# Out-degree counts folded chunk by chunk and the flag's matmul moved ahead of the last gates, in a two-layer graph kernel

## The chip, the cores and the metric

The kernel runs on one core of a Trainium2 chip. The metric is the device time of one execution in microseconds (us), as the median of several runs. The engines are named as in the profile: PE is TensorE (PEld its weight loads), DVE is VectorE, ACT is ScalarE, POOL is GpSimd, SP is the engine whose queue issues the DMAs.

## What is computed

The reference is two residual graph layers on 6250 nodes with 128 features and 206250 edges, sorted by destination. Cut to what matters:

```python
h = relu(layernorm(x))
deg = segment_sum(ones, src)                    # out-degree
x = x + relu(segment_sum((h * clip(deg, 1) ** -0.5)[src], dst)) @ W.T + b
h = relu(layernorm(x))
messages = segment_sum(h[src] @ W_msg.T + b_msg + edge_embed[type], dst)
x = x + gru_cell(messages, h, W_ih, W_hh, b_ih, b_hh)
```

The edge list holds each drawn edge in both directions and a loop for each node, so every node's out-degree is its in-degree. The kernel uses in-degrees (they are cheap to get from the sorted list) and verifies while it runs that they equal the out-degrees. If they don't, or another assumption on the list fails, a flag is set and a slow general path runs at the end. With these inputs it never runs.

## The kernel before, in words

The nodes are laid out on 125 partitions with 50 nodes each (`BLOCKS`), and the destination nodes are treated in 25 chunks (`CHUNKS`) of two nodes per partition, so 250 destinations (`CH`). For each chunk the kernel builds an adjacency tile in half precision, 50 source blocks by 250 destinations, from one-hot matrices (L698, L1063, L881), multiplies it with the layer's table (L1074) and writes it to a DRAM buffer. That is the first part of the run, up to about 640 us.

Layer 1 (`tensor_layer1`, `scalar_layer1`, `vector_layer1`, `sync_layer1`) reads the adjacency back in the order m = 0 to 24 (the last two chunks, which are still on the chip, come first). Each chunk is loaded into one of two slots of `ring` in four parts (`PARTS`, of 13, 13, 12 and 12 blocks, L417). PE multiplies all 50 blocks, each with a high and a low table (100 matmuls, L1196). Between part 1 and part 2 of chunk m it runs the gate matmuls of chunk m - 1 (`post1_gates_tensor`, L1162 to L1167, single precision), and after part 3 the two transposes of chunk m - 1 (`post1_turn_tensor`, L1173). ACT scales the aggregated messages (L1011) and does the sigmoids (L1018) and the tanh (L1021). DVE does the GRU's elementwise steps: `post1_gate_vector` (L789, L791), `post1_state_vector` (L796, L798, L800) and `post1_out_vector` (L805). SP writes each chunk's result out (L402).

In the same loop DVE adds the chunk's adjacency, part by part, into `counted`, 50 rows of 250 half-precision sums for each partition (`add_counts`, L778). A row belongs to one source node, so the sum over its 250 entries, over all chunks and over the partitions' share is that node's out-degree. The order on DVE is written out by hand: in iteration m the adds of parts 0 and 1 of chunk m, the gate step of chunk m - 1, the add of part 2, the state step of m - 1, the add of part 3, the out step of m - 1. The adds of parts 0 and 1 of the last chunk are pulled to the end of iteration 23. The load of chunk m + 2's part into a slot waits for PE's (`used1`) and DVE's (`added`) use of the part that is there.

After the loop DVE folds the 250 sums of a row to 124, 62 and 32 (L833, three adds), reduces them (L836), compares them with the degrees and collects all flags into `over` (L837 to L844). Only then does it take the gate step of the last chunk. PE has meanwhile done the last chunk's gate matmuls, waits for `mismatch`, sums the flags over the partitions by a one-column matmul (`psFlag`, L1208), and then waits for the last transposes. DVE turns the sum into an integer flag (L847), does the last state step and the last out step. All engines read the flag in `branch` and wait for the output DMAs.

A `Chain` is a helper by which DVE counts its own instructions on a semaphore; `ch.wait()` waits (L112) until all of them so far are done.

Of the kernel before, what the change touches and what calls it, by code (L numbers as in the profile page):

```python
# [7 lines left out]
ALU = mybir.AluOpType  # L8
ACT = mybir.ActivationFunctionType
AX = mybir.AxisListType.X  # L10
# [5 lines left out]
P = slice(0, LO)  # L16
# [3 lines left out]
CH = CB * LO  # L20
CHUNKS = N // CH
# [21 lines left out]
CAND = HLEN + 64  # L43
# [7 lines left out]
PARTS = [(0, 13), (13, 26), (26, 38), (38, BLOCKS)]  # L51
# [10 lines left out]
used0 aggr psX x1 pvar pstd pnm h1 psT hst psM tab_hi psF tab_lo h1T_out  # L62
used1 added h1c_in0 h1c_in1 msg psRZ psN rz nin nn hnew psO result out
load0_0 load0_1 load0_2 load0_3 load1_0 load1_1 load1_2 load1_3
mismatch flag_sum flag_set v_chain
Gflat_in Gx_in Gxb Gh0 Gdeg Gdeg_root Gconst Gtab_zero Gsum_zero Gemb_out Gh0_scaled Gtable_out Gtable1_out
Ghist Ghot Gerows Gturned0 Gturned1 Gsum_in0 Gsum_in1 Gadded0 Gadded1 Gindex Grows0 Grows1 Gsums
Gdiag Gacross Gsame Gproduct
# [50 lines left out]
def gnn(nc, x, edges, dst, dst_heads, w0t, b0, wmt, bm, emb, wiht, whht, bih, bhh, out):  # L119
# [3 lines left out]
    def sem(name):  # L123
        return sems[name]
# [7 lines left out]
    with ctx:  # L132
# [8 lines left out]
        ring = sb("ring", [128, 2, SLOTS * CH], F16)  # L141
# [46 lines left out]
        over = sb("over", [128, CHUNKS], F32)  # L188
# [149 lines left out]
        def slot(m):  # L338
            return (m + 1) % 2
# [428 lines left out]
            post0_x_vector(v, ch, CHUNKS - 2)  # L768
            post0_norm_vector(v, ch, CHUNKS - 2)

        def add_counts(v, m, j):

            a, b = (CH * k for k in PARTS[j])
            part, into = ring[P, slot(m), a:b], counted_n[P, a:b]
            if m >= 2:
                v.wait_ge(sem(f"load{slot(m)}_{j}"), 16 * (m // 2))
                v.wait_ge(sem("added"), 4 * (m - 1) + j + 1)
                v.tensor_tensor(into, into, part, ALU.add).then_inc(sem("added"), 1)  # L778
            elif m == 1:
                v.wait_ge(sem("added"), j + 1)  # L780
                v.tensor_tensor(into, into, part, ALU.add).then_inc(sem("added"), 1)
            else:
                v.tensor_copy(into, part).then_inc(sem("added"), 1)

        def post1_gate_vector(v, ch, m):
            v.wait_ge(sem("psN"), m + 1)
            v.wait_ge(sem("rz"), m + 1)
            positive(v, sem("nn"), m)
            ch.did(v.scalar_tensor_tensor(nin, psN[:, 1, :], bg_h[:, 2:3], rz[:, 0, :], ALU.add, ALU.mult))  # L789
            ch.wait()  # L790
            v.tensor_tensor(nin, nin, psN[:, 0, :], ALU.add).then_inc(sem("nin"), 1)  # L791

        def post1_state_vector(v, ch, m):
            v.wait_ge(sem("nn"), m + 1)
            positive(v, sem("psO"), m)
            ch.did(v.tensor_tensor(hnew, h1c[:, m % 2, :], nn, ALU.subtract))  # L796
            ch.wait()
            ch.did(v.tensor_tensor(hnew, rz[:, 1, :], hnew, ALU.mult))  # L798
            ch.wait()
            v.tensor_tensor(hnew, nn, hnew, ALU.add).then_inc(sem("hnew"), 1)  # L800

        def post1_out_vector(v, m):
            q = chunk(m)
            v.wait_ge(sem("psO"), m + 1)
            v.tensor_tensor(x_sb[P, blocks(q), :], psO, x_sb[P, blocks(q), :], ALU.add).then_inc(sem("result"), 1)  # L805

        def vector_layer1(v, ch):
            last = CHUNKS - 1
            v.wait_ge(sem("built"), UNITS * CHUNKS)
            for m in range(CHUNKS):  # L810
                if m == 0:
                    add_counts(v, m, 0)
                    post0_x_vector(v, ch, last)
                    post0_norm_vector(v, ch, last)
                    for j in range(1, 4):
                        add_counts(v, m, j)
                    check_sorted(v, ch)
                    continue
                if m < last:
                    add_counts(v, m, 0)  # L820
                    add_counts(v, m, 1)
                post1_gate_vector(v, ch, m - 1)
                add_counts(v, m, 2)
                post1_state_vector(v, ch, m - 1)
                add_counts(v, m, 3)
                post1_out_vector(v, m - 1)
                if m == last - 1:
                    add_counts(v, last, 0)
                    add_counts(v, last, 1)

            v.wait_ge(sem("added"), 4 * CHUNKS)
            for to, other in ((124, 126), (62, 64), (32, 32)):
                ch.did(v.tensor_tensor(counted_v[P, :, 0:to], counted_v[P, :, 0:to], counted_v[P, :, other:other + to],  # L833
                                       ALU.add))
                ch.wait()
            ch.did(v.tensor_reduce(outdeg[P, :], counted_v[P, :, 0:32], AX, ALU.add))  # L836
            ch.did(v.tensor_reduce(flags[P, 0:1], over[P, :], AX, ALU.max))  # L837
            ch.did(v.tensor_scalar(flags[P, 3:4], flags[P, 3:4], float(CAND), None, ALU.is_ge))
            ch.wait()
            ch.did(v.tensor_tensor(outdeg[P, :], outdeg[P, :], deg[P, :], ALU.not_equal))  # L840
            ch.wait()
            ch.did(v.tensor_reduce(flags[P, 2:3], outdeg[P, :], AX, ALU.max))
            ch.wait()
            v.tensor_reduce(over[P, 0:1], flags[P, :], AX, ALU.add).then_inc(sem("mismatch"), 1)  # L844
            post1_gate_vector(v, ch, last)
            v.wait_ge(sem("flag_sum"), 1)
            v.tensor_scalar(flag_i[:, :], psFlag, 0.0, None, ALU.is_gt).then_inc(sem("flag_set"), 1)  # L847
            post1_state_vector(v, ch, last)
            post1_out_vector(v, last)

# [303 lines left out]
        def post1_gates_tensor(pe, m):  # L1154
            pe.wait_ge(sem("msg"), m + 1)
            positive(pe, sem("rz"), m)
            positive(pe, sem("nin"), m)
            pe.wait_ge(sem(f"h1c_in{m % 2}"), 16 * (m // 2 + 1))
            h = h1c[:, m % 2, :]
            for a in range(2):  # L1160
                w = slice(D * a, D * (a + 1))
                pe.matmul(psRZ[:, a, :], wih_sb[:, w], msgs, start=True, stop=False)  # L1162
                last = pe.matmul(psRZ[:, a, :], whh_sb[:, w], h, start=False, stop=True)  # L1163
            last.then_inc(sem("psRZ"), 1)
            w = slice(2 * D, 3 * D)
            pe.matmul(psN[:, 0, :], wih_sb[:, w], msgs, start=True, stop=True)  # L1166
            pe.matmul(psN[:, 1, :], whh_sb[:, w], h, start=True, stop=True).then_inc(sem("psN"), 1)  # L1167

        def post1_turn_tensor(pe, m):
            pe.wait_ge(sem("hnew"), m + 1)  # L1170
            positive(pe, sem("result"), m)
            for j in range(CB):
                last = pe.transpose(psO[:, j, :], hnew[:, LO * j:LO * (j + 1)], ident[:, :])  # L1173
            last.then_inc(sem("psO"), 1)
# [3 lines left out]
        def tensor_layer1(pe):  # L1178
            pe.wait_ge(sem("emb_in"), 16 * TA)
            pe.wait_ge(sem("types_moved"), 32)  # L1180
            pe.wait_ge(sem("tab_lo"), CHUNKS - 1)
            for m in range(CHUNKS):
                bank = (CHUNKS + m) % 2
                if m:
                    positive(pe, sem("msg"), m - 1)
                else:
                    pe.wait_ge(sem("aggr"), CHUNKS - 1)
                for j, (a, b) in enumerate(PARTS):
                    if m >= 2:
                        pe.wait_ge(sem(f"load{slot(m)}_{j}"), 16 * (m // 2))  # L1190
                    for h in range(a, b):
                        K = 128 if h < TB else LO
                        if m == 0 and h == CB * (CHUNKS - 1):
                            pe.wait_ge(sem("tab_lo"), CHUNKS)
                        for s in range(2):
                            last = pe.matmul(psD[bank], tabv[1][0:K, h, s, :], adj[slot(m)][0:K, h, :],  # L1196
                                             start=h == 0 and s == 0, stop=h == BLOCKS - 1 and s == 1)
                        if h == b - 1:
                            last.then_inc(sem("used1"), 1)
                        if m == 0 and h in LAST0:  # L1200
                            LAST0[h](pe, CHUNKS - 1)
                    if m and j == 1:
                        post1_gates_tensor(pe, m - 1)
                    if m and j == 3:
                        post1_turn_tensor(pe, m - 1)
            post1_gates_tensor(pe, CHUNKS - 1)
            pe.wait_ge(sem("mismatch"), 1)
            pe.matmul(psFlag, over[P, 0:1], ones[P, 0:1], start=True, stop=True).then_inc(sem("flag_sum"), 1)  # L1208
            post1_turn_tensor(pe, CHUNKS - 1)


# [361 lines left out]
```

## Time and profile before

| | us |
|---|---|
| three runs: median (lowest to highest) | 997.35 (994.53 to 997.53) |
| the profiled execution's own time | 993.72 |
| its span in the profile | 991.9 |
| PE busy | 852.4 (86%) |
| DVE busy | 808.3 (81%) |
| ACT busy | 515.5 (52%) |
| mean granted TensorE clock | 0.975 |

The span is the stretch from the first to the last recorded instruction, and 1.8 us of the execution's own time lie outside it. A granted clock of 1.00 is 2.4 GHz, and 0.50 is 1.2 GHz. In the views below a row of a timeline gives the start, the duration (of all instructions of a merged row together), engine, line, operation, what is written and read, how many (x) and in brackets the idle time of the engine before it with what ended it.

### The profile page before, as it was taken

The page shows a single profiled execution, that of the slowest core. Times are in us where ns is not written, and L with a number is a line of the kernel's source. Part 1 is how long each engine was busy: PE and PEld are TensorE (multiplying, and loading weights), DVE is VectorE, ACT ScalarE, POOL GpSimd, SP SyncE. Part 2 cuts the span into 40 slices and gives each one's busy share as a digit, 9 for nine tenths or more (in the row PEclk, how much of TensorE's full clock was granted, in tenths as well). Part 3 has the DMA queues.
Part 4 walks back from the last instruction along what each step waited for, and adds up shares of the span by engine and source line. Part 5 has one row for each costly group of instructions (what it writes and reads, how often), then busy time and mean ns, then how long its engine had stood idle before and what let it go on. Part 6 is the DMA issues. An engine that isn't in the chain of part 4 may idle for free.

```text
span 991.9 us, 21125 instructions
## 1 busy us (share of the span) xinstructions
PE 852.4 (86%) x8908; PEld 758.8 (77%) x8908; DVE 808.3 (81%) x1177; ACT 515.5 (52%) x1051; POOL 74.4 (8%) x71
## 2 busy tenths in 40 slices
PE   1333599898998998989989999989999999999993
PEld 1222488787887887878878888969888889888882
DVE  5959999999999999999999995267766667766666
ACT  2896278687886886868868887211111111111110
POOL 5860100100101001000000000000000000000000
PEclk9999889999999999999999999999999999999997
DMA  4623315443434544333534330266667776666740
GB/s 108 143 68 130 132 50 221 159 159 136 159 141 159 227 174 159 137 137 147 212 134 187 140 141 7 60 237 242 245 245 266 280 269 245 241 246 260 280 162 12
DMA packets 38739, 169.99 MB, mean 171 GB/s; under 512 B 8156, under 2 KB 21667, under 8 KB 35696
## 3 DMA queue, kind: packets, MB, share of 16 engines
q1 hardware_dynamic: 32486, 161.48, 43.2%
q0 software_dynamic: 6000, 6.48, 2.8%
q8 instruction: 71, 1.16, 0.5%
q10 hardware_dynamic: 154, 0.64, 0.2%
q14 instruction: 28, 0.23, 0.1%
HBM read 88.52 MB, written 80.00 MB: 170 GB/s over the span
## 4 chain that ended last, share of the span: by engine, by line
PE 55%; DVE 29%; ACT 11%; issue 3%; DMA 2%; SPq 0%; DVEq 0%
PE ps L1196 25%; PE ps L1074 13%; DVE work L691 9%; DVE work L698 7%; PE ps L1063 7%; ACT ring L881 5%; DVE work L704 2%; PE ps L1162 2%; PE ps L1163 2%; ACT junk L893 2%; DMA tab<-dst 1%; PE ps L1086 1%; PE ps L1167 1%; PE ps L1166 1%; PE ps L1100 1%
## 5 line engine op out<-in xcount | busy, mean ns | idle before, releaser
L1063 PE MATMUL ps<-work 128*128 128x106 f16 x3125 | 437.2, 217 | 86.4 <-ACT ring L881 66.9
L1074 PE MATMUL ps<-ring,tab 125*128 125x250 f16 x2500 | 422.1, 275 | 1.9 <-DVE tab L676 1.2
L881 ACT ACTIVATE ring<-ps 128x848 f16<-128x848 f32 x375 | 330.0, 882 | 98.1 <-PE ps L1063 92.2
L1063 PEld LDWEIGHTS ps<-work 128*128 128x128 f16 x3125 | 291.4, 102 | 108.0 <-ACT ring L881 67.2
L1196 PE MATMUL ps<-ring,tab 125*128 125x250 f16 (+1 forms) x2500 | 277.0, 269 | 0.0
L1074 PEld LDWEIGHTS ps<-ring,tab 125*128 125x128 f16 x2500 | 246.9, 99 | 28.5 <-DVE tab L676 1.5
L1196 PEld LDWEIGHTS ps<-ring,tab 125*128 125x128 f16 (+1 forms) x2500 | 242.6, 97 | 28.8 <-issue 0.3
L691 DVE TENSOR_TENSOR work<-iota_lo,mch 128x3150 f16<-128x3150 f16 x125 | 224.4, 1795 | 26.0 <-PE ps L1063 13.6
L698 DVE TENSOR_TENSOR work<-iota_w,mch 128x1250 f16<-128x1250 f16 x250 | 193.9, 817 | 0.0
L778 DVE TENSOR_TENSOR work<-work,ring 125x3250 f16<-125x3250 f16 (+1 forms) x92 | 161.8, 1779 | 0.0
L1018 ACT ACTIVATE raw<-ps,bg 128x250 f32<-128x250 f32 x50 | 20.7, 466 | 174.9 <-PE ps L1163 174.9
L789 DVE SCALAR_TENSOR_TENSOR raw<-ps,bg_h,raw 128x250 f32<-128x250 f32 x25 | 11.9, 477 | 96.0 <-PE ps L1167 96.0
L704 DVE TENSOR_TENSOR work<-iota_t,mch_s 128x225 f16<-128x225 f16 x125 | 65.9, 527 | 0.0
L463 POOL DMA_INDIRECT raw<-edges,run_i x25 | 37.6, 1502 | 353.5 <-DVE fields L564 287.5
L1011 ACT ACTIVATE raw<-ps,ginv 128x250 f32<-128x250 f32 x25 | 11.8, 470 | 86.8 <-PE ps L1196 86.8
L921 ACT ACTIVATE h1s<-x_sb,pnm,prs 125x128 f32<-125x128 f32 x50 | 23.9, 482 | 24.1 <-DVE pnm L725 24.1
L456 POOL DMA_INDIRECT ring<-dst,row_i x25 | 33.5, 1342 | 16.0 <-DVE row_i L508 8.7
L1162 PE MATMUL ps<-raw,wih_sb 128*128 128x250 f32 x100 | 29.9, 380 | 3.6 <-DMA raw<-h_turned 3.2
L1021 ACT ACTIVATE raw<-raw,bg_i 128x250 f32<-128x250 f32 x25 | 12.6, 504 | 35.5 <-DVE raw L791 35.5
L1163 PE MATMUL ps<-raw,whh_sb 128*128 128x250 f32 x100 | 29.7, 378 | 0.0
L712 DVE TENSOR_TENSOR x_sb<-ps,x_sb 125x256 f32<-125x256 f32 x25 | 12.2, 490 | 20.2 <-PE ps L1088 20.2
L1086 PE MATMUL ps<-w_sb,aggr 128*125 128x128 f32 x100 | 17.1, 294 | 9.3 <-ACT tab L940 9.3
(156 smaller groups left out, 608.9 us busy)
## 6 DMA issues: line engine op xcount, KB each, us to landing
adjacency<-ring SPq DMA_DIRECT2D x23, 2937.5 KB
ring<-adjacency SPq DMA_DIRECT2D x46, 812.5 KB, 6.3
ring<-adjacency SPq DMA_DIRECT2D x46, 750.0 KB, 8.8
adjacency<-ring SPq DMA_DIRECT2D x23, 183.1 KB
h_turned<-hst SPq DMA_DIRECT2D x25, 125.0 KB, 2.0
raw<-h_turned SPq DMA_DIRECT2D x25, 125.0 KB, 2.0
out<-x_sb SPq DMA_DIRECT2D x25, 125.0 KB
x_sb<-x SPq DMA_DIRECT2D x4, 560.0 KB
```

The lines of the kernel that those rows point to most:

```text
L456: gp.indirect_dma_start(cand[P, g, :], None, dst.rearrange("(a n) -> a n", a=1), bass.IndirectOffsetOnAxis(row_i[P, g:g + 1], 1))\
L463: gp.indirect_dma_start(raw[P, g % RAW, :], None, edges.rearrange("(a n) k -> a (n k)", a=1), bass.IndirectOffsetOnAxis(run_i[P, g:g + 1], ...
L691: ch.did(v.tensor_tensor(lohot[:, s, :, 0:even].rearrange("p k (n t) -> p k n t", t=2), iota_lo[:, 0:even].rearrange("p (n t) -> p n t", t ...
L698: ch.did(v.tensor_tensor(combo[:, s, :, cols].rearrange("p k (n t) -> p k n t", t=2), iota_w[:, cols].rearrange("p (n t) -> p n t", t=2).u ...
L704: v.tensor_tensor(typehot[:, s, :, :, :], iota_t[:, :, :].unsqueeze(1).broadcast_to([128, BATCH, 1 + WIN, TB]), mch_s[:, par, :, at, :].re ...
L778: v.tensor_tensor(into, into, part, ALU.add).then_inc(sem("added"), 1)
L881: act.activation(to(x * 2 * u, 2, x), ps[:, s:s + 2, 0:x * SLOTS].rearrange("p b (x h) -> p h b x", h=SLOTS), ACT.Copy).then_inc(sem("evac ...
L1063: last = pe.matmul(ps[:, 2 * (u % 2) + i // BANKW, o:o + WCOLS], lohot[:, s, k, :], combo[:, s, k, :], start=True, stop=True)
L1074: mm = pe.matmul(psD[c % 2], tabv[0][P, h, s, :], adj[c % 2][P, h, :], start=i == 0, stop=i == 2 * BLOCKS - 1)
L1162: pe.matmul(psRZ[:, a, :], wih_sb[:, w], msgs, start=True, stop=False)
L1163: last = pe.matmul(psRZ[:, a, :], whh_sb[:, w], h, start=False, stop=True)
L1196: last = pe.matmul(psD[bank], tabv[1][0:K, h, s, :], adj[slot(m)][0:K, h, :], start=h == 0 and s == 0, stop=h == BLOCKS - 1 and s == 1)
```

## The change

The out-degree sums are folded earlier and in other places.

- Iteration 22 ends with the first fold, 250 to 126 columns (`fold_counts`, 124 added), over what chunks 0 to 22 have summed.
- In iteration 23 each add of a part becomes two, 126 and 124 columns wide, both into the first 126 columns, the second waiting for the first by the new semaphore `narrow`. The iteration ends with the second fold, to 64 columns, and then all of chunk 24 is added (`add_last_counts`): four passes of 64, 64, 64 and 58 columns over the four parts, 16 adds, where before two of its four adds stood here.
- Iteration 24 (DVE's last steps for chunk 23) holds no adds. Its gate step is followed by the third fold, to 32 columns, its state step by the comparison (`compare_degrees`), then comes its out step, the integer flag, and then all of chunk 24's steps.
- PE waits for the comparison and does the flag's matmul ahead of the last chunk's gate matmuls, no longer behind them.

```diff
@@ -62,7 +62,7 @@
 used0 aggr psX x1 pvar pstd pnm h1 psT hst psM tab_hi psF tab_lo h1T_out
 used1 added h1c_in0 h1c_in1 msg psRZ psN rz nin nn hnew psO result out
 load0_0 load0_1 load0_2 load0_3 load1_0 load1_1 load1_2 load1_3
-mismatch flag_sum flag_set v_chain
+mismatch narrow flag_sum flag_set v_chain
 Gflat_in Gx_in Gxb Gh0 Gdeg Gdeg_root Gconst Gtab_zero Gsum_zero Gemb_out Gh0_scaled Gtable_out Gtable1_out
 Ghist Ghot Gerows Gturned0 Gturned1 Gsum_in0 Gsum_in1 Gadded0 Gadded1 Gindex Grows0 Grows1 Gsums
 Gdiag Gacross Gsame Gproduct
@@ -768,19 +768,57 @@
             post0_x_vector(v, ch, CHUNKS - 2)
             post0_norm_vector(v, ch, CHUNKS - 2)
 
-        def add_counts(v, m, j):
-
-            a, b = (CH * k for k in PARTS[j])
-            part, into = ring[P, slot(m), a:b], counted_n[P, a:b]
+        def add_counts(v, m, j, width=CH):
+
+            first, end = PARTS[j]
             if m >= 2:
                 v.wait_ge(sem(f"load{slot(m)}_{j}"), 16 * (m // 2))
+            if m == 0:
+                a, b = CH * first, CH * end
+                v.tensor_copy(counted_n[P, a:b], ring[P, slot(m), a:b]).then_inc(sem("added"), 1)
+                return
+            if width == CH:
+                a, b = CH * first, CH * end
                 v.wait_ge(sem("added"), 4 * (m - 1) + j + 1)
-                v.tensor_tensor(into, into, part, ALU.add).then_inc(sem("added"), 1)
-            elif m == 1:
-                v.wait_ge(sem("added"), j + 1)
-                v.tensor_tensor(into, into, part, ALU.add).then_inc(sem("added"), 1)
-            else:
-                v.tensor_copy(into, part).then_inc(sem("added"), 1)
+                v.tensor_tensor(counted_n[P, a:b], counted_n[P, a:b], ring[P, slot(m), a:b], ALU.add)\
+                 .then_inc(sem("added"), 1)
+                return
+            into, rest = counted_v[P, first:end, 0:width], CH - width
+            v.tensor_tensor(into, into, adj[slot(m)][P, first:end, 0:width], ALU.add).then_inc(sem("narrow"), 1)
+            v.wait_ge(sem("narrow"), j + 1)
+            into = counted_v[P, first:end, 0:rest]
+            v.tensor_tensor(into, into, adj[slot(m)][P, first:end, width:CH], ALU.add).then_inc(sem("added"), 1)
+
+        def add_last_counts(v, m, width):
+            for k, at in enumerate(range(0, CH, width)):
+                for j, (first, end) in enumerate(PARTS):
+                    if k == 0:
+                        v.wait_ge(sem(f"load{slot(m)}_{j}"), 16 * (m // 2))
+                    else:
+                        v.wait_ge(sem("narrow"), 4 * k + j + 1)
+                    n = min(width, CH - at)
+                    into = counted_v[P, first:end, 0:n]
+                    ins = v.tensor_tensor(into, into, adj[slot(m)][P, first:end, at:at + n], ALU.add)
+                    ins.then_inc(sem("narrow" if at + n < CH else "added"), 1)
+
+        def fold_counts(v, ch, m, to, other):
+
+            v.wait_ge(sem("added"), 4 * (m + 1))
+            ch.did(v.tensor_tensor(counted_v[P, :, 0:to], counted_v[P, :, 0:to], counted_v[P, :, other:other + to],
+                                   ALU.add))
+            ch.wait()
+
+        def compare_degrees(v, ch):
+
+            ch.did(v.tensor_reduce(outdeg[P, :], counted_v[P, :, 0:32], AX, ALU.add))
+            ch.did(v.tensor_reduce(flags[P, 0:1], over[P, :], AX, ALU.max))
+            ch.did(v.tensor_scalar(flags[P, 3:4], flags[P, 3:4], float(CAND), None, ALU.is_ge))
+            ch.wait()
+            ch.did(v.tensor_tensor(outdeg[P, :], outdeg[P, :], deg[P, :], ALU.not_equal))
+            ch.wait()
+            ch.did(v.tensor_reduce(flags[P, 2:3], outdeg[P, :], AX, ALU.max))
+            ch.wait()
+            v.tensor_reduce(over[P, 0:1], flags[P, :], AX, ALU.add).then_inc(sem("mismatch"), 1)
 
         def post1_gate_vector(v, ch, m):
             v.wait_ge(sem("psN"), m + 1)
@@ -817,34 +855,27 @@
                     check_sorted(v, ch)
                     continue
                 if m < last:
-                    add_counts(v, m, 0)
-                    add_counts(v, m, 1)
-                post1_gate_vector(v, ch, m - 1)
-                add_counts(v, m, 2)
-                post1_state_vector(v, ch, m - 1)
-                add_counts(v, m, 3)
-                post1_out_vector(v, m - 1)
+                    width = 126 if m == last - 1 else CH
+                    add_counts(v, m, 0, width)
+                    add_counts(v, m, 1, width)
+                    post1_gate_vector(v, ch, m - 1)
+                    add_counts(v, m, 2, width)
+                    post1_state_vector(v, ch, m - 1)
+                    add_counts(v, m, 3, width)
+                    post1_out_vector(v, m - 1)
+                if m == last - 2:
+                    fold_counts(v, ch, m, 124, 126)
                 if m == last - 1:
-                    add_counts(v, last, 0)
-                    add_counts(v, last, 1)
-
-            v.wait_ge(sem("added"), 4 * CHUNKS)
-            for to, other in ((124, 126), (62, 64), (32, 32)):
-                ch.did(v.tensor_tensor(counted_v[P, :, 0:to], counted_v[P, :, 0:to], counted_v[P, :, other:other + to],
-                                       ALU.add))
-                ch.wait()
-            ch.did(v.tensor_reduce(outdeg[P, :], counted_v[P, :, 0:32], AX, ALU.add))
-            ch.did(v.tensor_reduce(flags[P, 0:1], over[P, :], AX, ALU.max))
-            ch.did(v.tensor_scalar(flags[P, 3:4], flags[P, 3:4], float(CAND), None, ALU.is_ge))
-            ch.wait()
-            ch.did(v.tensor_tensor(outdeg[P, :], outdeg[P, :], deg[P, :], ALU.not_equal))
-            ch.wait()
-            ch.did(v.tensor_reduce(flags[P, 2:3], outdeg[P, :], AX, ALU.max))
-            ch.wait()
-            v.tensor_reduce(over[P, 0:1], flags[P, :], AX, ALU.add).then_inc(sem("mismatch"), 1)
-            post1_gate_vector(v, ch, last)
+                    fold_counts(v, ch, m, 62, 64)
+                    add_last_counts(v, last, 64)
+            post1_gate_vector(v, ch, last - 1)
+            fold_counts(v, ch, last, 32, 32)
+            post1_state_vector(v, ch, last - 1)
+            compare_degrees(v, ch)
+            post1_out_vector(v, last - 1)
             v.wait_ge(sem("flag_sum"), 1)
             v.tensor_scalar(flag_i[:, :], psFlag, 0.0, None, ALU.is_gt).then_inc(sem("flag_set"), 1)
+            post1_gate_vector(v, ch, last)
             post1_state_vector(v, ch, last)
             post1_out_vector(v, last)
 
@@ -1203,9 +1234,9 @@
                         post1_gates_tensor(pe, m - 1)
                     if m and j == 3:
                         post1_turn_tensor(pe, m - 1)
-            post1_gates_tensor(pe, CHUNKS - 1)
             pe.wait_ge(sem("mismatch"), 1)
             pe.matmul(psFlag, over[P, 0:1], ones[P, 0:1], start=True, stop=True).then_inc(sem("flag_sum"), 1)
+            post1_gates_tensor(pe, CHUNKS - 1)
             post1_turn_tensor(pe, CHUNKS - 1)
```

## Rows read from the trace of the kernel before

**Rows 1.** Chain of waits that ended last: start, us, engine, tile, line
```profile
966.59 0.49 DVE raw L789
...
972.35 3.30 DVE work L833
975.68 1.78 DVE work L833
977.49 1.00 DVE work L833
978.51 1.82 DVE outdeg L836
...
981.11 0.49 DVE raw L789
...
984.81 0.42 DVE x_sb L805
```

**Rows 2.** Timeline of PE, the last two turns, the last gates, the flag
```profile
957.98 0.38 PE L1173 MATMUL ps<-ident,raw 128*125 128x128 f32 x2
...
971.47 0.38 PE L1173 MATMUL ps<-ident,raw 128*125 128x128 f32 x2
972.19 0.69 PE L1162 MATMUL ps<-raw,wih_sb 128*128 128x250 f32 x2 [0.34 <-ACT raw L1011]
...
974.40 0.58 PE L1167 MATMUL ps<-raw,whh_sb 128*128 128x250 f32 x2
981.21 0.19 PE L1208 MATMUL ps<-ones,over 125*1 125x1 f32 x2 [6.22 <-DVE over L844]
983.98 0.79 PE L1173 MATMUL ps<-ident,raw 128*125 128x128 f32 x2 [2.58 <-DVE raw L800]
```

**Rows 3.** Timeline of DVE, iterations 23 and 24 and the comparison's end
```profile
945.28 3.61 DVE L778 TENSOR_TENSOR work<-work,ring 125x3250 f16<-125x3250 f16 x2
953.10 0.48 DVE L789 SCALAR_TENSOR_TENSOR raw<-ps,bg_h,raw 128x250 f32<-128x250 f32 x1 [4.21 <-PE ps L1167]
...
956.81 1.71 DVE L778 TENSOR_TENSOR work<-work,ring 125x3000 f16<-125x3000 f16 x1
958.44 0.42 DVE L805 TENSOR_TENSOR x_sb<-ps,x_sb 125x256 f32<-125x256 f32 x1
958.77 3.60 DVE L778 TENSOR_TENSOR work<-work,ring 125x3250 f16<-125x3250 f16 x2
...
981.00 0.16 DVE L844 TENSOR_REDUCE over<-flags 125x1 f32<-125x4 f32 x1
```

**Rows 4.** Timeline of SP, issue of chunk 24's loads
```profile
944.26 1.99 SPq L417 DMA_DIRECT2D ring<-adjacency  x4
```

**Rows 5.** DMA issues from 944 us on: count, KB each, us to landing
```profile
ring<-adjacency SPq DMA_DIRECT2D x2, 750.0 KB, 9.1
```

**Rows 6.** Timeline of ACT, tanh of chunk 23 and sigmoids of chunk 24
```profile
967.55 0.50 ACT L1021 ACTIVATE raw<-raw,bg_i 128x250 f32<-128x250 f32 x1 [1.05 <-DVE raw L791]
...
974.18 0.83 ACT L1018 ACTIVATE raw<-ps,bg 128x250 f32<-128x250 f32 x2 [2.04 <-PE ps L1163]
```

**Rows 7.** Stretches: length, PE, PEld, DVE, ACT, POOL busy, clock, DMA share, GB/s
```profile
108.00:109.00 1.00, 0.43 (x6) 0.43 (x7) 1.00 (x1) 1.00 (x2) 0.00 (x0) 0.76 0.00 0
978.00:979.00 1.00, 0.00 (x0) 0.00 (x0) 0.97 (x2) 0.00 (x0) 0.00 (x0) 0.96 0.00 0
```

**Rows 8.** Timeline of PE, two pauses in the build
```profile
107.24 0.73 PE L1063 MATMUL ps<-work 128*128 128x106 f16 x12 [1.31 <-DVE work L704]
...
114.37 2.32 PE L1074 MATMUL ps<-ring,tab 125*128 125x250 f16 x20 [1.24 <-DVE tab L676]
```

**Rows 9.** Timeline of PE, the first gate matmuls of layer 1
```profile
650.25 0.66 PE L1162 MATMUL ps<-raw,wih_sb 128*128 128x250 f32 x2 [3.24 <-DMA raw<-h_turned]
...
652.76 1.04 PE L1166 MATMUL ps<-raw,wih_sb 128*128 128x250 f32 x2
653.60 1.04 PE L1167 MATMUL ps<-raw,whh_sb 128*128 128x250 f32 x2
```

## The prediction

> **What bounds the kernel now.** I read the chain of waits that ended last first. Up to 966.5 us it runs through PE in every iteration of layer 1, so adds on DVE cost nothing there; DVE stands idle 4.21 us before each gate step [rows 3]. Behind that it goes over to DVE: from the gate step of chunk 23 at 966.59 through the three folds, the reduction and the comparison to chunk 24's gate step at 981.11 and the last out step, which ends at 984.81 + 0.42 = 985.23 [rows 1]. PE's timeline shows the other side: the last gate matmuls are done at 974.40 + 0.58 = 974.98, and PE then idles 6.22 us until DVE has `over` ready [rows 2]. So 981.11 - 974.98 = 6.1 us is all that any reordering of DVE's work can give, and the change has to keep its new work off the stretch behind 966.6, where DVE already is the bound.
>
> **Prices.** The three dependent folds start at 972.26 (0.09 before the chain's 972.35, since DVE starts an independent instruction 0.33 us after one of 0.42), 975.68 and 977.49, and the reduction at 978.51 [rows 1, 3]. From 3100 and 1600 columns in 1.81 and 1.02 us comes (1.81 - 1.02) / 1500 = 0.52 ns for a column of a half-precision add, with 0.18 us on top for each instruction behind which the next one waits. An independent successor starts about 0.11 sooner (0.33 after one of 0.42 instead of 0.02 behind its end), so 0.07 on top. The 125x3000 add of 1.71 us [rows 3] is 1.56 + 0.15, which fits. I take these prices for the narrow adds too: the folds have rows of 62 and 32 columns and go at the same rate.
>
> **Iterations 22 and 23.** The first fold takes the place at 945.28 [rows 3]: 6200 x 0.52 + 0.18 = 3.4, to 948.7. Each part of 13 blocks is 1638 columns (0.85 + 0.18, since its second half waits) and 1612 (0.84 + 0.07), 1.94 in all and twice, to 952.6. The gate step waits for PE until 953.10 [rows 3], so 3.4 + 0.3 us more work lies in the 4.21 us of idle time and costs nothing; without that cover it would cost 3.7. The adds of 12 blocks take 1.81 where they took 1.63 (956.81 to 958.44), so the state step ends by 957.1, ahead of the turn at 957.98 [rows 2], and the out step starts at 958.82 instead of 958.44. No load is touched: the last four are issued at 944.26, behind adds that stand as before [rows 4], and land some 9.1 us later [rows 5], before the first pass over chunk 24 at 961. The h1 load behind the state step starts 0.2 us later and isn't needed before 972.
>
> **The stretch that decides.** From 958.82 DVE works without a pause.
> - Out step 0.33, second fold 3100 x 0.52 + 0.18 = 1.79: 960.94.
> - The 16 adds of chunk 24: 12500 x 0.52 = 6.50, and 16 x 0.07 = 1.12, because each waits for one four places ahead of it, long done. 7.62: 968.56. Before, the two adds here were done by 962.4 and gates waited for PE until 966.59. So chunk 23's gate step comes 1.97 late.
> - Gate step 0.84, third fold (1600 columns, 1.01): 970.41. The tanh, 0.96 behind the gate step's start and 0.50 long [rows 6], is done at 970.02 and not waited for.
> - State step, two starts of 0.45 and a third of 0.42: done at 971.73. PE's turn, at 971.47 before [rows 2], is 0.3 late. The next step of the comparison starts at 971.64.
> - Reduction and comparison, 981.00 - 978.51 = 2.49 to the start of the last one [rows 1, 3]: 974.13. The flag's matmul starts 0.21 behind (981.21 against 981.00 [rows 2, 3]): 974.34.
> - The moved matmul itself now stands ahead of the gates. No row shows it followed by another: between 0 and its full 0.19, I take 0.16, so the gate matmuls start at 974.5 instead of 972.19. Out step and integer flag run beside them.
> - With the clock at 2.4 GHz the sigmoids start 974.18 - 972.19 = 1.99 behind, last 0.83 [rows 2, 6], and DVE starts 0.1 later: chunk 24's gate step at 977.42 instead of 981.11, **3.7 us earlier**. The rest is as before: 4.12 us to the end of the last out step, and the same output and branch behind it. No add, no fold and no comparison is removed; they are only moved to where DVE waits.
>
> **The clock.** The new order leaves PE without work between the turn (done at 972.2) and the flag's matmul at 974.34, 2.2 us in place of a pause behind all the gates. Before, the granted clock went down at 978.9 (mean 0.96 in that stretch [rows 7]), 3.9 us after PE's last gate matmul. Rows that are nearer to 2.2 us point both ways. Behind a pause of 1.31 us and 0.7 us of matmuls the clock fell within 108 to 109 us [rows 7, 8]. Behind one of 1.24 us, with dense work ahead of it, I read no fall [rows 8]. In the first gates of layer 1, behind 3.24 us, it fell when two of the six pairs were through, and a pair then took 653.60 - 652.76 = 0.84 us [rows 9] where one takes (974.40 - 972.19) / 5 = 0.44 now [rows 2]. So the price is between 0 and 6 x 0.42 = 2.5 us, and the fall does not have a fixed distance from the pause. A pause of 2.2 us with only two transposes shortly ahead of it is longer than the 1.31 that sufficed, so I take a fall, on average with a bit over a third of the gates done: 1.6 us. The last turn is then at the low clock, as before (0.79 against 0.38 [rows 2]).
>
> **Sum.** 3.7 - 1.6 = 2.1 us. Against the profiled execution, 993.72 - 2.1 = 991.6; the median of the runs shown is 3.6 above that execution, 997.35 - 2.1 = **995.3**. About 0.3% (3.0 us) is what a measurement of this kernel can tell from no change.
>
> **The rivals.**
> 1. The clock holds through the gates (2.2 us is shorter than the 3.24 of rows 9). The gain is 3.7, and up to 0.41 more if the last turn finds it high too: 993.3 to 993.65.
> 2. Each of the 16 adds pays the dependent price, 0.18 in place of 0.07. The stretch from 958.8 on has no slack, so the gates come 16 x 0.11 = 1.8 us later. Gain 1.9 with the high clock, 0.3 with the mean fall, -0.6 with the whole of it: 995.4 to 998.0. For it speaks that every one has a wait ahead of it; against it, that the adds before have two waits each and still two of 3250 columns take 3.61 [rows 3], 6500 x 0.52 = 3.38 and 0.23 for both. Here the Trainium skill speaks against the change: "VectorE: DVE Perf Modes", on the errata of instructions that read SBUF, says that many small tiles each pay an exposed latency. This is the same mechanism, but these rows show most of it hidden between independent adds. The page's own formula, an overhead of 151 cycles at 0.96 GHz or 0.16 us for each operation, would be an estimate of 1.4 us more for the 16.
> 3. **Slower:** adds of 64-column pieces out of rows of 250 run at one column per cycle as the reduction does (1600 columns in 1.74 us). The 16 then take 12500 x 1.04 + 1.1 = 14.1 instead of 7.6, and every step behind them comes 6.5 late: 2.8 slower than before with the high clock, 4.4 with the mean fall, so 1000.2 to 1001.7. It decides from 3.7 / 16 = 0.23 us more for an add on. Against it are the folds, with rows as short and the same stride; for it only that no row shows this very shape.
> 4. The moved work is in no one's way before either and nothing changes. It would need PE to be done later than DVE at the end; rows 2 exclude it.
>
> **The chances.** Forecast (the clock falls somewhere in or before the gates, gain 1.1 to 3.2): 0.55. Rival 1: 0.27. Rival 2: 0.12. Rival 3: 0.04. Rival 4 and things unseen: 0.02. The forecast's own range is 994.1 to 996.3. The whole one takes in rival 1, most of rival 2 and half of the 3 us over which the runs before scatter: 992.3 to 998.0. Faster by over 3.0 us is rival 1 for the most part and the upper end of the forecast, 0.32; slower is rival 3 and a bit of rival 2, 0.05; the rest, 0.63, is within 0.3%.
>
> **What would show it.** In the changed profile: the first fold ending by 952.6 with its adds and a gate step still waiting for PE at 953.1; sixteen adds in 7.6 us (0.43 to 0.51 from start to start) behind 961, and chunk 23's gate step near 968.6 without idle time; the flag's matmul near 974.3, and gates behind it. Then the granted clock from 972 to 980 decides between the forecast and rival 1: gate pairs of 0.44 or of 0.84. DVE should idle some 2.5 us or more ahead of chunk 24's gate step, waiting for PE or ACT. Wrong would be a pause of DVE anywhere between 958.8 and 974.3, adds of 0.6 us or more, or PE waiting in the loop before 971.5.

## The result and the profile after

| | before | changed |
|---|---|---|
| median of ten runs (lowest to highest), us | 996.37 (994.53 to 997.53) | 993.60 (992.59 to 995.39) |
| the profiled execution's own time | 993.72 | 995.39 |
| its span | 991.9 | 993.5 |
| DVE busy | 808.3 | 809.8 |

The ratio is 0.9976, with an interval of 0.9968 to 0.9984: 2.4 us faster, between 1.6 and 3.2. The profiled execution of the changed kernel happens to be the slowest of its ten, and that of before, 993.72, is faster than any of the ten of before. In the changed kernel's trace layer 1 begins later (PE's first gate matmul at 653.91 against 650.25 [rows 9]), and chunk 22's turn is at 961.63 against 957.98 [rows 2], as much later; on PE the turns ahead of it are 13.5 us apart in both. So from here on times are counted from the start of chunk 22's turn to the end of the last out step. I call this stretch the **tail**. It is 985.23 - 957.98 = 27.25 us before.

The chain of waits that ended last, changed kernel (start, us, engine, tile, line; L801 are the 16 adds, L807 the folds, L813 the reduction, L827 the gate step, L1238 the flag's matmul, L1193 to L1198 the gate matmuls):

```profile
962.82 1.78 DVE work L807
964.60 0.02 issue
964.62 6.02 DVE work L801 x13
970.64 0.28 issue
970.92 1.41 DVE work L801 x3
972.33 0.40 DVE raw L827
...
975.43 1.73 DVE outdeg L813
...
978.04 0.19 PE ps L1238 x2
978.23 0.03 issue
978.26 1.02 PE ps L1193 x2
979.28 0.83 PE ps L1194 x2
980.12 0.83 PE ps L1193 x2
980.95 0.83 PE ps L1194 x2
981.78 0.51 PE ps L1197 x2
982.29 0.43 PE ps L1198 x2
982.73 0.03 issue
982.75 0.49 DVE raw L827
...
986.46 0.42 DVE x_sb L843
```

Against [rows 1], the folds and the reduction of chunk 24 no longer stand right ahead of the last gate step. In their place stand the gate matmuls, which were no part of the chain before. The tail is 986.46 + 0.42 - 961.63 = 25.25 us, 2.0 less than before, and within the interval of the runs. DVE's timeline shows where it waits:

```profile
956.75 0.48 DVE L827 SCALAR_TENSOR_TENSOR raw<-ps,bg_h,raw 128x250 f32<-128x250 f32 x1 [0.40 <-ACT raw L1049]
...
964.62 7.71 DVE L801 TENSOR_TENSOR work<-work,ring 125x832 f16<-125x832 f16 x16
972.24 0.47 DVE L827 SCALAR_TENSOR_TENSOR raw<-ps,bg_h,raw 128x250 f32<-128x250 f32 x1
...
977.83 0.16 DVE L821 TENSOR_REDUCE over<-flags 125x1 f32<-125x4 f32 x1
...
982.75 0.48 DVE L827 SCALAR_TENSOR_TENSOR raw<-ps,bg_h,raw 128x250 f32<-128x250 f32 x1 [4.34 <-PE ps L1198]
```

The pause of 4.21 us ahead of chunk 22's gate step [rows 3] has shrunk to 0.40: the first fold went into it and the step is not late. But there are now 4.34 us ahead of the last gate step, in which DVE waits for the gate matmuls that the change put behind the comparison. PE's timeline and the stretches around them (the columns as in rows 7):

```profile
975.49 0.48 PE L1204 MATMUL ps<-ident,raw 128*125 128x128 f32 x2 [0.20 <-DVE raw L838]
978.04 0.19 PE L1238 MATMUL ps<-ones,over 125*1 125x1 f32 x2 [2.07 <-DVE over L821]
978.26 1.02 PE L1193 MATMUL ps<-raw,wih_sb 128*128 128x250 f32 x2
979.08 1.04 PE L1194 MATMUL ps<-raw,whh_sb 128*128 128x250 f32 x2
```

```profile
977.00:978.00 1.00, 0.00 (x0) 0.00 (x0) 0.90 (x7) 0.00 (x0) 0.00 (x0) 1.00 0.00 0
978.00:979.00 1.00, 0.93 (x4) 0.78 (x5) 0.42 (x2) 0.00 (x0) 0.00 (x0) 0.71 0.00 0
979.00:980.00 1.00, 1.00 (x4) 0.77 (x3) 0.00 (x0) 0.00 (x0) 0.00 (x0) 0.50 0.29 83
...
981.00:982.00 1.00, 1.00 (x4) 0.82 (x4) 0.00 (x0) 0.18 (x1) 0.00 (x0) 0.58 0.00 0
982.00:983.00 1.00, 0.71 (x4) 0.30 (x2) 0.25 (x1) 0.65 (x2) 0.00 (x0) 1.00 0.00 0
...
985.00:986.00 1.00, 0.37 (x1) 0.37 (x2) 0.54 (x2) 0.00 (x0) 0.00 (x0) 0.62 0.00 0
```

The granted clock goes to half at 978.4, behind a pause of 2.07 us and just after the gates have begun, and is back at 981.8, with four of the six pairs through. It falls a second time at 985.2, ahead of the last turn, which takes 0.79 us as before. The pairs are 0.83 apart while it is low, and the six take 982.71 - 978.26 = 4.45 us where they took 2.79 [rows 2].

### The profile page after: what moved, and what is told of

Same layout as the page of the kernel before. It is cut to its first block, busy times and chain, and to the rows that moved or that the text cites. A ratio compares the mean times of both kernels' runs of the same rounds, so it can differ in the third digit from the quotient of the medians.

```text
span 993.5 us, 21135 instructions
## 1 busy us (share of the span) xinstructions
PE 857.2 (86%) x8908; PEld 761.6 (77%) x8908; DVE 809.8 (82%) x1193; ACT 515.4 (52%) x1051; POOL 77.1 (8%) x71
## 4 chain that ended last, share of the span: by engine, by line
PE 54%; DVE 29%; ACT 11%; issue 3%; DMA 3%; SPq 0%; DVEq 0%
PE ps L1227 24%; PE ps L1105 13%; DVE work L691 9%; DVE work L698 7%; PE ps L1094 7%; ACT ring L912 5%; DVE work L704 2%; PE ps L1193 2%; PE ps L1194 2%; ACT junk L924 2%; DMA tab<-dst 1%; PE ps L1117 1%; PE ps L1131 1%; PE ps L1197 1%; PE ps L1198 1%
## 5 line engine op out<-in xcount | busy, mean ns | idle before, releaser
L691 DVE TENSOR_TENSOR work<-iota_lo,mch 128x3150 f16<-128x3150 f16 x125 | 224.5, 1796 | 28.1 <-PE ps L1094 16.5
L783 DVE TENSOR_TENSOR work<-work,ring 125x3250 f16<-125x3250 f16 (+1 forms) x88 | 154.8, 1780 | 0.0
L827 DVE SCALAR_TENSOR_TENSOR raw<-ps,bg_h,raw 128x250 f32<-128x250 f32 x25 | 11.9, 477 | 92.3 <-PE ps L1198 91.9
L463 POOL DMA_INDIRECT raw<-edges,run_i x25 | 40.4, 1615 | 353.2 <-DVE fields L564 285.4
L1193 PE MATMUL ps<-raw,wih_sb 128*128 128x250 f32 x100 | 31.0, 394 | 4.2 <-DMA raw<-h_turned 4.2
L890 ACT ACTIVATE mch<-ps 128x250 f16<-128x250 f32 x50 | 18.3, 371 | 13.5 <-PE ps L1083 13.5
```

The source lines that it names most:

```text
L463: gp.indirect_dma_start(raw[P, g % RAW, :], None, edges.rearrange("(a n) k -> a (n k)", a=1), bass.IndirectOffsetOnAxis(run_i[P, g:g + 1], ...
L691: ch.did(v.tensor_tensor(lohot[:, s, :, 0:even].rearrange("p k (n t) -> p k n t", t=2), iota_lo[:, 0:even].rearrange("p (n t) -> p n t", t ...
L783: v.tensor_tensor(counted_n[P, a:b], counted_n[P, a:b], ring[P, slot(m), a:b], ALU.add)\
```

## The experiments

**Is the flag's place what costs? Folding alone, and the flag's part alone.** These two runs and the two given kernels make the four combinations of the change's two parts.

```diff
 # folding alone: the changed kernel, with
-            pe.wait_ge(sem("mismatch"), 1)
-            pe.matmul(psFlag, over[P, 0:1], ones[P, 0:1], ...).then_inc(sem("flag_sum"), 1)
             post1_gates_tensor(pe, CHUNKS - 1)
+            pe.wait_ge(sem("mismatch"), 1)
+            pe.matmul(psFlag, over[P, 0:1], ones[P, 0:1], ...).then_inc(sem("flag_sum"), 1)
```

> The changed kernel with the order on PE put back: last gates first, then the wait for the comparison and the flag's matmul. The tail is counted from the start of chunk 22's turn to the end of the last out step: 27.25 us before, 25.25 in the changed kernel. Theory (the moved matmul makes DVE idle 4.34 us ahead of the last gate step, the folding alone is the gain): the gates follow the turn of chunk 23, at the high clock, the last gate step comes 3.9 us earlier, tail 21.3, the kernel 6.0 us (0.6%) below before. Rival (the gates would be as late or as slow in either place, and the folding alone gives all that there is): tail 25 to 25.3, 2 us below before.

```diff
 # the flag's part alone: the kernel before, with
-            post1_gates_tensor(pe, CHUNKS - 1)
             pe.wait_ge(sem("mismatch"), 1)
             pe.matmul(psFlag, over[P, 0:1], ones[P, 0:1], ...).then_inc(sem("flag_sum"), 1)
+            post1_gates_tensor(pe, CHUNKS - 1)
...
-            post1_gate_vector(v, ch, last)
             v.wait_ge(sem("flag_sum"), 1)
             v.tensor_scalar(flag_i[:, :], psFlag, ...).then_inc(sem("flag_set"), 1)
+            post1_gate_vector(v, ch, last)
```

> The kernel before with only the flag's part of the change: on PE the flag's matmul ahead of the last gates, on DVE the integer flag ahead of the last gate step; all adds and folds as before. Theory: PE waits for the comparison until about 23.2 us of the tail, the clock has fallen by then, six gate pairs take 5 us, and the last gate step is 5.7 us late: tail 32.9, 5.7 us (0.6%) slower than before. If the clock cost nothing: tail 30.4, 3.2 us slower. Rival (the flag's place is harmless): tail 27.3.

Each ratio is to runs of the kernel before that were taken beside it.

| tail, us (ratio to before, interval) | adds and folds as before | folded chunk by chunk |
|---|---|---|
| last gates, then the flag | 27.25 | 21.09 (0.9930, 0.9917 to 0.9944) |
| the flag, then the last gates | 32.55 (1.0041, 1.0025 to 1.0056) | 25.25 (0.9976, 0.9968 to 0.9984) |

Folding alone takes 6.2 us off the tail, and the flag's move gives 4.2 of it back. The move also costs 5.3 on its own. Both came out near what the theory had (21.3 and 32.9 were expected). The run with the flag's part alone, PE and then DVE's last gate step:

```profile
984.56 0.19 PE L1207 MATMUL ps<-ones,over 125*1 125x1 f32 x2 [9.36 <-DVE over L844]
984.77 1.17 PE L1162 MATMUL ps<-raw,wih_sb 128*128 128x250 f32 x2
...
989.75 0.48 DVE L789 SCALAR_TENSOR_TENSOR raw<-ps,bg_h,raw 128x250 f32<-128x250 f32 x1 [4.82 <-PE ps L1167]
```

PE of the run with folding alone:

```profile
974.52 0.48 PE L1204 MATMUL ps<-ident,raw 128*125 128x128 f32 x2 [0.20 <-DVE raw L838]
974.89 0.69 PE L1193 MATMUL ps<-raw,wih_sb 128*128 128x250 f32 x2
...
977.10 0.58 PE L1198 MATMUL ps<-raw,whh_sb 128*128 128x250 f32 x2
977.62 0.19 PE L1239 MATMUL ps<-ones,over 125*1 125x1 f32 x2
980.83 0.48 PE L1204 MATMUL ps<-ident,raw 128*125 128x128 f32 x2 [3.03 <-DVE raw L838]
```

The gates run beside the reduction and the comparison, at full clock. DVE's last gate step there starts at 977.95 and had waited 0.49 us, for the flag's matmul. The rival, that folding can't give more than the changed kernel shows, is out.

**Is the clock's fall from the pause?** Unread matmuls go between chunk 23's turn and the wait for the comparison, 18 of them and, in a second run, 9.

```diff
+            for i in range(18):
+                pe.matmul(psD[0], tabv[1][P, i, 0, :], adj[slot(CHUNKS - 1)][P, i, :], start=True, stop=True)
             pe.wait_ge(sem("mismatch"), 1)
```

> The changed kernel with 18 half-precision matmuls of 250 columns, whose results nobody reads, between the turn of chunk 23 and the wait for the comparison, some 1.95 us in a pause of 2.07. Theory (the clock fell because of the pause, and cost 1.66 us of the gates' 4.45): granted clock 1.00 through the gates, pairs start 0.44 apart, tail 23.6, 3.7 us (0.4%) below before. Rival (the fall has to do with something else, such as the single-precision matmuls): pairs 0.83 apart, tail 25.25 or, if the added matmuls delay the flag's, up to 25.7.

> The changed kernel with 9 instead of 18 of the unread matmuls behind chunk 23's turn, so a pause of some 1.1 us is left. If a pause must be nearly 2 us to bring the clock down: gates at the high clock, tail 23.6. If the share of work around it decides, the clock may still fall in part, as it did behind the pause of 1.31 us of the kernel before: tail up to 26.1. I give the first two chances in three.

With 18, PE:

```profile
975.07 2.12 PE L1238 MATMUL ps<-ring,tab 125*128 125x250 f16 x18
977.30 0.19 PE L1240 MATMUL ps<-ones,over 125*1 125x1 f32 x2
977.52 0.66 PE L1193 MATMUL ps<-raw,wih_sb 128*128 128x250 f32 x2
...
979.70 0.58 PE L1198 MATMUL ps<-raw,whh_sb 128*128 128x250 f32 x2
```

Its clock in the gates (columns as in rows 7):

```profile
978.00:979.00 1.00, 1.00 (x6) 0.90 (x5) 0.00 (x0) 0.00 (x0) 0.00 (x0) 1.00 0.20 53
```

The pairs are 0.42 apart, the granted clock stays at 1.00 and the tail is 23.31 us (ratio to before 0.9954, interval 0.9939 to 0.9970). With 9, a pause of 1.09 us is left; the clock holds through the gates too and the tail is 23.31 as well (one execution):

```profile
978.78 0.19 PE L1240 MATMUL ps<-ones,over 125*1 125x1 f32 x2 [1.09 <-DVE over L821]
```

So the fall comes from the work that is missing in that pause. Whether the length of the pause decides or the work around it, these two runs don't show; in the kernel before, 1.31 us with little work around them had sufficed [rows 7, 8]. The fall costs 1.66 us in the gates (1.63 at DVE's last gate step), and the high clock gives another 0.31 in the last turn (0.48 for 0.79), together the 1.94 by which the tails differ. Of the 4.2 us that the flag's move gave back, these 1.9 are the clock's, and 23.31 - 21.09 = 2.2 are the order's alone.

**Is the place of the fall a matter of chance?** Three more profiled executions of the changed kernel as it is.

> The changed kernel as it is, once more, for a second look at the same pause. Theory (where the clock falls against the end of the pause is a matter of chance from one execution to the next, since nothing in the program sets it): the pause is 2.07 us again, DVE's rows stand at the same distances within 0.05 us, but the low stretch of the gates may be another, with a tail anywhere from 23.6 to 26.1 us. Rival (the program sets it): the same 4.45 us of gates and a tail of 25.25.

> A third look at the changed kernel as it is. In the first two the clock fell 16.8 and 17.05 us into the tail and tails were 25.25 and 25.26. If the place of the fall is a matter of chance, this look or the next should differ by more than 0.5 us in the fall; if something in the program sets it, both fall within 16.5 to 17.3 and the tail is 25.2 to 25.3.

> A fourth look at the changed kernel, with the same expectations as for the third.

The tails are 25.26, 25.23 and 25.23, and the clock fell 17.0 us into each (16.8 in the first execution). These executions took 993.08, 995.04 and 993.41, and their tails began at 959.29, 961.27 and 959.72, so 2 us of scatter upstream moves the fall along with the program. The theory, that the place would change by chance from one execution to the next, did not hold in these four: their falls lie within 0.25 us. What ties the fall to the program is not settled. It came 3.9 us behind the end of PE's last matmuls in the kernel before, 2.45 to 2.7 behind the end of chunk 23's turn here, and 0.6 behind it in the run with dependent adds that follows.

**What does an add pay for its wait?** The 16 adds in the order of the parts, so that each pass waits for the one just ahead.

```diff
-            for k, at in enumerate(range(0, CH, width)):
-                for j, (first, end) in enumerate(PARTS):
+            for j, (first, end) in enumerate(PARTS):
+                for k, at in enumerate(range(0, CH, width)):
...
-                        v.wait_ge(sem("narrow"), 4 * k + j + 1)
+                        v.wait_ge(sem("narrow"), 4 + 3 * j + k)
```

> The changed kernel with the 16 adds of the last chunk in another order: the four passes of a part directly behind each other, so that 12 of them wait for the one just ahead. Theory (an add pays 0.11 us more where the one just ahead must be finished, and nothing for a wait on an older one): the 16 take 7.7 + 12 x 0.11 = 9.0 us, tail 26.5. Rival (the wait itself has the price, whatever it waits for): 7.7 us, tail 25.25.

```profile
961.79 9.22 DVE L801 TENSOR_TENSOR work<-work,ring 125x832 f16<-125x832 f16 x16
970.93 0.47 DVE L827 SCALAR_TENSOR_TENSOR raw<-ps,bg_h,raw 128x250 f32<-128x250 f32 x1
```

From start to start of what follows, the 16 take 970.93 - 961.79 = 9.14 us instead of 972.24 - 964.62 = 7.62: 1.52 more, 0.127 for each of the 12. The theory holds, with 0.127 for 0.11, and so does the other half of it: the adds of the changed kernel wait as often and pay nothing. The tail is 27.32 and the ratio 1.0004 (0.9992 to 1.0016). That is 0.8 more than the 26.5 expected, and PE and its clock show why:

```profile
974.17 0.48 PE L1204 MATMUL ps<-ident,raw 128*125 128x128 f32 x2 [1.70 <-DVE raw L838]
976.72 0.19 PE L1238 MATMUL ps<-ones,over 125*1 125x1 f32 x2 [2.07 <-DVE over L821]
```

```profile
975.00:975.25 0.25, 0.00 (x0) 0.00 (x0) 0.25 (x1) 0.00 (x0) 0.00 (x0) 1.00 0.00 0
975.25:975.50 0.25, 0.00 (x0) 0.00 (x0) 0.25 (x1) 0.00 (x0) 0.00 (x0) 0.50 0.00 0
```

The later adds give PE a second pause, 1.70 us ahead of chunk 23's turn. The clock falls at 16.4 us of the tail, 0.6 us into the pause behind the turn and ahead of the gates, which all run low (5.3 us). It is high again in time for the last turn (0.51).

**A version beyond both.** From the run with the gates first: the three products with the old state, which need no message, go ahead of chunk 23's turn, and the integer flag goes behind the last gate step. The second run adds 18 unread matmuls ahead of the last turn.

```diff
+            post1_gate_vector(v, ch, last)
             v.wait_ge(sem("flag_sum"), 1)
             v.tensor_scalar(flag_i[:, :], psFlag, 0.0, None, ALU.is_gt).then_inc(sem("flag_set"), 1)
-            post1_gate_vector(v, ch, last)
...
+        def last_gates_old_state(pe, m):
...
+            for a in range(2):
+                w = slice(D * a, D * (a + 1))
+                pe.matmul(psRZ[:, a, :], whh_sb[:, w], h, start=True, stop=False, skip_group_check=True)
+            pe.matmul(psN[:, 1, :], whh_sb[:, 2 * D:3 * D], h, start=True, stop=True)
...
+                    if m == CHUNKS - 1 and j == 3:
+                        last_gates_old_state(pe, m)
                     if m and j == 3:
                         post1_turn_tensor(pe, m - 1)
+            last_gates_message(pe, CHUNKS - 1)
             pe.wait_ge(sem("mismatch"), 1)
```

> The changed kernel with the last gates ahead of the flag's matmul, their three products with the old state issued ahead of chunk 23's turn (they don't need the messages), and the integer flag behind the last gate step. In the run with the gates first, the last gate step started at 17.27 us of the tail, 0.27 behind the last gate matmul and held 0.49 by the integer flag. Theory (DVE is then the bound): it starts right behind chunk 23's out step, at 16.6, tail 20.4, 6.8 us below before. Rival (PE stays the bound there, because the split costs it what it saves): tail 20.9 to 21.1.

> The same as the run before it with 18 unread matmuls between the flag's matmul and the last turn. Theory: the turn takes 0.48 us, as in the run with the gates first, also where the clock would have fallen by then, so 0 to 0.31 us less than without: tail 20.4. Rival (the added matmuls hold up the turn): tail above 20.7.

DVE, and ACT's sigmoids ahead of it, in the first of the two:

```profile
976.13 0.83 ACT L1049 ACTIVATE raw<-ps,bg 128x250 f32<-128x250 f32 x2 [1.86 <-PE ps L1214]
976.36 0.41 DVE L843 TENSOR_TENSOR x_sb<-ps,x_sb 125x256 f32<-125x256 f32 x1
977.04 0.48 DVE L827 SCALAR_TENSOR_TENSOR raw<-ps,bg_h,raw 128x250 f32<-128x250 f32 x1 [0.27 <-issue]
```

The tail is 20.77 us (ratio 0.9935, 0.9921 to 0.9950), so 0.3 less than with the gates first instead of the 0.7 of the theory. PE had the gates done by 976.50, but the gate step starts 0.68 behind the out step and not 0.34. The profile puts the idle time before it down to issue, but ACT's rows show the wait: the step reads the two sigmoids, and they end at 976.13 + 0.83 = 976.96, 0.08 ahead of it. That is the distance at which it follows them where the profile names ACT (in the run with 18 unread matmuls 980.40 behind 979.48 + 0.83 = 980.31). So the bound is still PE's products with the message, followed by the sigmoids, which the theory left out, and not DVE. With the unread matmuls the tail is 20.76 and the ratio 0.9927 (0.9914 to 0.9940). The last turn took 0.48 us without them already, since the clock fell only 20.4 us in, just behind that turn, so they bought nothing. All three versions with the gates first beat both kernels; between them the runs can't choose.

## Why the prediction came out right

- **Bound and prices.** The expected places, counted in the tail, against the measured: second fold 1.17 and 1.19, the 16 adds 7.62 and 7.62 long, chunk 23's gate step 10.58 and 10.61, its turn 13.79 and 13.86, the flag's matmul 16.36 and 16.41, the gates 16.5 and 16.63. Not one step of the stretch that decides was off by more than 0.13 us. About half of it is the flag's own matmul, which holds the gates by 978.26 - 978.04 = 0.22 us, where I had taken 0.16 and at most 0.19. In iterations 22 and 23 none of the added work moved PE. The price of a column was divided out too low: (1.81 - 1.02) / 1500 is 0.53 and not 0.52. The 0.52 comes from the first and the third fold, (3.42 - 1.02) / 4600, so the sum stands.
- **The clock** was the uncertain term, put between 0 and 2.5 and taken as 1.6. It was 1.66, and that hit is luck. I took 1.6 as an average over places where the fall might lie, with a bit over a third of the gates done ahead of it. In the four executions the fall stands in one place, at the start of the gates, and the clock comes back when four pairs are through, which the sum didn't have. Some four pairs at the low clock is the price either way; had the clock stayed down, it would have been the 2.5 that the run with dependent adds shows (5.3 against 2.79). That the clock falls behind 2.2 us of pause was argued from the pause of 1.31 us that had sufficed [rows 7, 8]; the two runs with unread matmuls show that it is the work missing in the pause. The last turn is at the low clock, as forecast, but by a second fall.
- **Sum.** Expected 2.1 us less; the tail shows 2.0 and the runs 2.4 (1.6 to 3.2). The absolute 995.3 is 1.7 above the 993.60 measured. 1.0 of that is the median of before, which was 997.35 over three runs and is 996.37 over ten. So 993.60 lies in the whole range, 992.3 to 998.0, but under the forecast's own, 994.1 to 996.3, and where the first rival stood (993.3 to 993.65). The absolute time can't tell the two apart; the pairs 0.83 us apart and the tail of 25.25 do.
- **Rivals.** The first (clock holds, 3.7 to 4.1 gained) is what happens with the unread matmuls, 27.25 - 23.31 = 3.94. The second (dependent price) didn't come: 7.62 us for 12500 columns leave 0.07 for each add. By the estimate from the Trainium skill ("VectorE: DVE Perf Modes", on the errata), whose 151 cycles stand there for single-precision adds, they would have taken 9.0 us. The trace disagrees while an add waits for none of its near predecessors. In the run with dependent adds, 9.14 us in all, the 12 that wait pay some 0.20 each on top of their columns, against the page's 0.16. The third and the fourth rival are excluded by the same 7.62 and by the ratio.
- **What I didn't say.** The 4.3 us that DVE now idles were in my numbers (2.7 of them with the high clock), but I didn't draw the conclusion that the flag's move is a loss that folding pays for. The question to ask of the sum was what each part would give alone.

## What to carry to other kernels

Where a change has two parts, price each alone: moving sums off the end of the chain gave 6.2 us here, and putting a small matmul with a late input ahead of ready ones on the same engine took 4.2 of them away. Such a wait holds what stands behind it in the queue (2.2 of the 4.2 here), and the pause can cost the clock on top (1.9). When work is cut into many narrow adds, order them so that each waits for one several places back; the same adds then cost 0.07 us each on top of their columns, against some 0.20 when each needs the last.

## What the hardware showed that I hadn't expected

A pause of 2.07 us with two transposes ahead of it brought TensorE from 2.4 to 1.2 GHz in four executions out of four, at 16.8 to 17.0 us of the tail, although the tails began up to 2.3 us apart. A pause of 1.09 us in the same place didn't. With a pause of 1.70 us ahead of the two transposes as well, the clock fell 0.6 us into the one of 2.07.

Idle time that the profile calls issue can be a wait after all. In both runs with split gates the last gate step has 0.27 and 0.28 us of it, and starts 0.08 and 0.09 behind the end of ACT's sigmoids, which it reads.
